# Which unit of a group TensorE turns, when u is turned, and the order of a load and a transpose on SyncE

## The reference, cut to what matters

```python
x = x + layernorm(attention(layernorm(x)))       # only the last 516 tokens have a context
def bitlinear(x, w_latent):
    scale = clip(mean(abs(w_latent), axis=1), 1e-5)
    tern  = clip(round(w_latent / scale), -1, 1)
    return x @ (tern * scale).T
h = bitlinear(x, w_fc) + gate * (x @ v.T @ fast_b.T @ u.T)      # 1024 -> 4096, low rank 16
out = bitlinear(relu(h) ** 2, w_proj)                           # 4096 -> 1024
x = x + layernorm(out)
```

## Time and profile before

| | us |
|---|---|
| median of 3 runs | 1076.35 (1075.03 to 1078.9) |
| the profiled execution's own time | 1073.45 |
| its span, slowest core (core 2) | 1071.9 |
| spans of the eight cores | 1067.5 to 1071.9 |
| TensorE busy, core 2 | 1007.4 (94%) |
| VectorE, ScalarE, GpSimd busy, core 2 | 562.9, 361.5, 48.6 |

### The profile page before, as it was taken

One profiled execution on the slowest core, in us unless ns is written; L12 is line 12 of the kernel. 1 busy time (PEld: TensorE's weight loads), 2 busy tenths in 40 slices (PEclk: granted clock), 3 DMA queues, 4 the chain that ended last, 5 costly groups with the idle time before them and its releaser, 6 DMA issues.

```text
span 1071.9 us, 14984 instructions; the slowest of 8 cores (1067.5 to 1071.9 us)
## 1 busy us (share of the span) xinstructions
PE 1007.4 (94%) x4933; PEld 455.6 (43%) x4933; DVE 562.9 (53%) x813; ACT 361.5 (34%) x697; POOL 48.6 (5%) x105
## 2 busy tenths in 40 slices
PE   3688969999999999999999999999999999999997
PEld 1233334444444444444444444445444444444443
DVE  3679878745654545453445445633445353544333
ACT  4678788530003431143212341124301332013200
POOL 1111121000001000000000000000000000000000
PEclk9999889999999999999999999999999999999999
DMA  8699999942564125710455124622145401411021
GB/s 271 167 247 257 208 241 203 205 104 79 152 163 109 55 50 113 163 48 8 75 136 109 50 36 95 141 63 62 47 111 138 79 21 30 118 50 40 1 66 53
DMA packets 106367, 116.93 MB, mean 109 GB/s; under 512 B 82333, under 2 KB 82589, under 8 KB 106292
## 3 DMA queue, kind: packets, MB, share of 16 engines
q1 hardware_dynamic: 102324, 103.64, 38.7%
q0 software_dynamic: 3728, 12.25, 6.2%
q10 hardware_dynamic: 240, 0.07, 0.0%
HBM read 87.79 MB, written 17.31 MB: 98 GB/s over the span
## 4 chain that ended last, share of the span: by engine, by line
PE 82%; DVE 5%; issue 4%; DMA 4%; ACT 2%; POOL 1%; SPq 1%; ACTq 0%; DVEq 0%; POOLq 0%
PE pjp L649 38%; PE fcb L632 31%; PE pjp L632 2%; PE xp L799 1%; PE xp L649 1%; PE xp L762 1%; PE fcb L649 1%; DVE below L1443 1%; ACT rpp L1030 1%; PE pt L632 1%; DMA r<-v 1%; DMA Sfc<-tern 1%; ACT absd L1070 1%; PE pjp L696 1%; POOL rthr L521 1%
## 5 line engine op out<-in xcount | busy, mean ns | idle before, releaser
L632 PE MATMUL fcb<-xnT,Sfc 128*128 128x512 bf16 x1792 | 410.0, 386 | 8.1 <-DVE r L1425 4.9
L649 PE MATMUL pjp<-Spj,r 128*128 128x512 fp8e4 x1664 | 365.1, 379 | 1.7 <-DVE r2b L1425 1.7
L632 PEld LDWEIGHTS fcb<-xnT,Sfc 128*128 128x128 bf16 x1792 | 172.0, 99 | 229.0 <-issue 39.1
L1425 DVE TENSOR_TENSOR r<-fcb,rpp 128x512 bf16<-128x512 f32 x192 | 131.3, 690 | 224.7 <-ACT rpp L1030 224.5
L649 PEld LDWEIGHTS pjp<-Spj,r 128*128 128x128 bf16 x1664 | 160.5, 98 | 194.5 <-issue 5.0
L1030 ACT ACTIVATE rpp<-fcb,hsc 128x512 f32<-128x512 f32 x192 | 130.4, 686 | 208.5 <-PE fcb L632 199.3
L993 ACT ACTIVATE lv<-mv,cvecs 128x1 f32<-128x1 f32 x64 | 18.7, 293 | 281.2 <-DVE mv L1370 204.8
L1360 DVE TENSOR_TENSOR xy<-pjp,oscb 128x512 f32<-128x512 f32 x60 | 41.3, 689 | 130.2 <-PE pjp L649 130.2
L649 PE MATMUL pjp<-Spj,r2b 128*128 128x512 fp8e4 x256 | 55.4, 379 | 0.0
L1365 DVE BATCH_NORM_STATS2 s<-xy 128x6 f32<-128x512 f32 x64 | 44.4, 694 | 9.4 <-DVE xy L1360 6.0
L632 PE MATMUL pjp<-xnT,Sfc 128*128 128x512 bf16 x176 | 42.0, 390 | 6.2 <-ACT rpp L1030 4.7
(11 more groups left out here) (181 smaller groups left out, 704.8 us busy)
## 6 DMA issues: line engine op xcount, KB each, us to landing
xy<-x SPq DMA_DIRECT2D x31, 512.0 KB, 4.4
out<-xy SPq DMA_DIRECT2D x31, 512.0 KB, 3.0
xs<-x SPq DMA_DIRECT2D x25, 512.0 KB, 4.6
xy<-wfc SPq DMA_DIRECT2D x16, 512.0 KB, 5.8
xy<-wpj SPq DMA_DIRECT2D x16, 512.0 KB, 5.9
stg<-wfc SPq DMA_DIRECT2D x10, 512.0 KB, 6.0
stg<-wpj SPq DMA_DIRECT2D x8, 512.0 KB, 4.9
xs<-wpj SPq DMA_DIRECT2D x8, 512.0 KB, 5.4
```

What stands on the lines that cost most here:

```text
L632: mm = te.matmul(bank, s_fc[:, dci * HF + hc * 128:dci * HF + hc * 128 + 128], xnT[:, dci * TT:(dci + 1) * TT], start=(dci == 0), stop=(dc ...
L649: mm = te.matmul(dst, squares(j)[:, hc * TT + s * 128: hc * TT + s * 128 + 128], spj_even[:, hc // 2, hc % 2, half * 512:half * 512 + 512] ...
L1425: ve.tensor_tensor(squares(j)[:, hc * TT:(hc + 1) * TT], bank, rpp[n % 2][:], ALU.mult).then_inc(v_r2, 1)
```

## The change

- `BY_PE` holds units 1, 5, ... 29 and 31: nine units in place of eight, and of each group the second in place of the fourth.
- In TensorE's steps 4, 8, ... 24, `ut` comes behind `low_rank(n + 3)` and not ahead of it.
- ScalarE copies a unit that TensorE has turned behind the step's `abssum` and not ahead of it.
- SyncE issues the load into a slot ahead of the transpose of the unit that freed it, for all units.
- The first 16 chunks stand in steps 35 to 47 and not 37 to 47.

```diff
-BY_PE = [n for n in range(NFU) if n % 4 == 3]
+BY_PE = [n for n in range(NFU) if n % 4 == 1 or n == NFU - 1]
...
-    CHUNKS[37 + 11 * c // 16 if c < 16 else 17 + 2 * c if c < 20 else 36 + c
+    CHUNKS[35 + 13 * c // 16 if c < 16 else 17 + 2 * c if c < 20 else 36 + c
...
                 sync.wait_ge(v_ab, m + 1)
-                turned(m)
                 if m in AFTER:
                     wload(AFTER[m])
+                turned(m)
...
                 if n == 0:
                     low_rank(2)
-                if n == 1 or (n > 1 and n % GRP == 0 and n + 4 < NFU):
-                    ut(n // GRP + 1)
+                if n == 1:
+                    ut(1)
                 if n + 3 < NFU:
                     low_rank(n + 3)
+                if n > 1 and n % GRP == 0 and n + 4 < NFU:
+                    ut(n // GRP + 1)
...
-                if n in BY_PE:
-                    evac(n)
                 if n in STATS:
                     rstd1(STATS[n])
...
                 for u in SUMS[n]:
                     abssum(u)
+                if n in BY_PE:
+                    evac(n)
```

## The result

Over four runs of each in turn on one chip, the kernel after took 1088.87 us in the median (1086.96 to 1089.65) and the kernel before 1077.2 (1075.03 to 1078.9). The ratio is 1.0107, with a 95% interval of 1.0083 to 1.0131: 11.7 us slower, where 4.0 had been forecast. A few executions of every kernel here are some per cent longer, with a lower clock on the cores of a die; the ratios and the means leave them out. The profiled execution took 1088.99.

What follows compares the result with a forecast made beforehand. Bound: a TensorE stream of fixed length from step 48, whose start VectorE's cuts set. On core 2, 4.6 - 1.1 - 0.9 + 1.0 = +3.6, plus 0.4 for the slowest core: +4.0, median 1080.4 us; 8-in-10 range 1070 to 1088.

Steps and rivals of the forecast that it cites:

- The stream behind step 48 is of fixed length: TensorE from step 48 on, 887.1 us on core 2: time lost ahead of it arrives at the end almost whole.
- Unit 12: VectorE's cut of unit 12 on core 2 comes at 67.0 instead of 70.41, 3.4 us gained; less on other cores.
- The series copy, unit, `fc`, low rank product: Four statistics groups: TensorE's unit waits for ScalarE's late copy of u; 13.5 us against 12.67, 0.85 us lost in each.
- The clock: 1.9 a group: TensorE's 3.1 us gap in each of four groups lowers the clock for a short spell, costing 1.9 us a group.
- Units 28 to 33, 1.1 gained: Unit 33's stop shrinks with one transpose less on the queue: 1.1 us gained, bounds 2.5 gained and 1 lost.
- 33 to 47, 0.9 gained: Chunks two steps sooner: units 33 to 47 take 38.5 us instead of 39.4, bounds 3 gained and 4 lost.
- Behind unit 47: 1.0 lost: Unit 47's transpose is issued 0.57 later, behind a 512 KB load: 1.0 us lost, bounds 0.6 and 2.5.
- The rival that built on it: `w_proj` part: transposes behind loads land 1.5 us later, stopping every third cut, 6.5 us more, 1086.9; chance 0.10.
- The slowest of eight: +0.4: At the end, all cores finish near core 2, the slowest 0.4 us above the mean.
- The clock holds: Rival: 3.1 us gaps in the four groups leave the clock alone, -4.0 us, 1072.3; chance 0.22.
- The copy in time: Rival: ScalarE's copy of u is not late, groups stay at 12.67, -7.5 us, 1068.9; chance 0.08.
- All cancels: Rival: unit 12's gain offsets 0.85 and half the spells, within a microsecond or two of before, 1077; chance 0.10.

Runs made afterwards that it cites:

- experiment 12: Kernel after, with one `fc` product repeated ahead of TensorE's unit in steps 13, 17, 21, 25 and the products of chunks 14 and 15 repeated: ratio 1.0029 to before.
- Experiment 11: Kernel before with the first 16 chunks in steps 35 to 47 and the products of chunks 14 and 15 made once more: ratio 1.0024 to before.
- experiment 10: Kernel before with only the first 16 chunks moved to steps 35 to 47: ratio 1.0047 to before.
- Experiment 4: Kernel after with the `fc` of unit n - 2 repeated ahead of TensorE's unit in steps 13, 17, 21, 25: 1081.4 us, ratio 1.0035 to before.
- experiment 2: Kernel before with only SyncE's load issued ahead of the transpose: ratio 1.0023 to before.
- experiment 8: Kernel before with the load ahead of the transpose, except for units 45, 46 and 47: ratio 0.9997 to before.
- experiment 3: Kernel after with ScalarE's `rstd1` at the end of its step, behind the copy of u: 1080.89 us, ratio 1.0020 to before.
- experiment 5: Kernel after with the first 16 chunks back in steps 37 to 47: ratio 1.0101 to before.
- experiment 1: Kernel after with SyncE's order and the chunks as before, leaving unit choice, `ut` order and ScalarE's copy changed: 1087.22 us, ratio 1.0087 to before.
- experiment 6: Kernel before with only u's turn moved behind the low rank product: 1075.73 us, ratio 0.9968 to before.
- experiment 7: Kernel after with TensorE's unit at the end of its step, behind `fc` and the low rank product: 1082.89 us, ratio 1.0048 to before.

## Why the prediction was right in its mechanism and wrong in its size

**The stream behind step 48 is of fixed length: wrong by 3 us.** I had said that a microsecond lost ahead of step 48 arrives at the end almost whole. It does, but the tail grew as well, from 887.1 to 890.1 us on core 2 and by 3.2 in the mean. On core 2, 1.5 us of the 3.0 are the two products at step 48 (their starts take 190.25 to 195.18, 4.93 for 3.45), and 1.3 are clock lost between 340 and 350 us, which no run ties to the change (last section). In the mean the two products make 1.9 of the 3.2. Over the kernels of the table it follows the wait at step 48: 888.5 to 889.6 us in the six where that wait is below 2 us, 890.4 and 890.5 where it is 3.1 and 3.4, 891.0 to 891.9 in the five where it is 5.0 to 6.4 (experiment 12, with 2.2 and 890.9, lost clock elsewhere as well). The two products themselves are longer by 0.0 to 0.4 us in the mean of the cores in those six, by 1.4 in the two and by 1.9 to 2.4 in the five. On core 4 the two products behind the wait are 3.57 + 2.96 for 1.89 + 1.89, 2.8 us more. Experiment 11 did nothing but fill this wait in experiment 10, and the lost clock and the tail went down with it. I had priced the later transpose as 1.0 us of delay and had not asked what a wait of 5 us does to the clock, though I had just asked that of the groups.

**Unit 12: 3.4 us gained, 67.0.** On core 2 it was cut at 65.05, 5.4 sooner; in the mean of the cores 1.8, as the forecast said of the others.

**The series copy, unit, `fc`, low rank product.** Right as a mechanism: gaps ahead of the unit in all 32 places (four groups on eight cores), each ended by the copy of u. Their sizes are 2.84 to 4.43 us for a forecast of 3.1; on six cores the first is the longest. 63.6 us in the mean, and 63.55 on core 2, stand where I had 61.8. (Four times 13.5 and 1.9 is 61.6 or 61.7 and not 61.8; that slip changes nothing.) Experiment 4, with the clock held, has 55.6, 13.9 for a group against my 13.5. With the clock, the first group of core 4 is 66.19 to 82.69, 16.5: the statistics end 7.2 behind the cut and not 6.75, since VectorE stops for 0.39 us on `Sfc<-tern` ahead of them, and the copy ends 3.8 behind them and not 3.54.

**The clock: 1.9 a group.** Right: 8.0 us over four groups, 2.0 each, by after less experiment 4. I took it that all four gaps of a core lower it; 27 of 32 did, so one that did cost 2.4 (8.0 x 8 / 27), and that two errors cancel here is luck again. The other five, all of 3.03 or 3.04 us, were followed by `fc` at 1.89, as on core 2:

```profile
109.58 0.61 PE L714 MATMUL pt<-identb,tern 128*128 128x128 bf16 x8 [3.04 <-ACT uTs L1088]
110.03 1.89 PE L632 MATMUL fcb<-xnT,Sfc 128*128 128x512 bf16 x8
```

So "none above 2.5 did" is not a bound: it held for the 7 gaps of before and fails for 5 of 32. Nor does the length alone decide: a gap of 3.03 us on core 4 was followed by the low clock, and so were gaps of 1.85 and 1.89 us of before (cores 5 and 6), below the range that I had counted. The spell on core 4 runs from 77.49 to 81.85, 4.4 us. By the rule of the Trainium skill, TensorE: Matmul & The Clock Gate, section "HAM oscillation — how this bites in real kernels", that a spell costs half its length, this is 2.2; the rows give (0.81 - 0.46) + (3.55 - 1.82) = 2.1 between starts, so trace and rule agree, and my lower estimate by it had too short a spell.

**Unit 28 at 128.8: right.** Core 2 has 128.60. That two errors cancelled there (unit 12 two us sooner, the groups two longer) is luck.

**Units 28 to 33, 1.1 gained, and 33 to 47, 0.9 gained.** On core 2, 0.6 and 0.8 gained (14.94 and 38.56; forecast for the latter 38.5). In the mean of the cores 0.5 gained and 0.2 lost.

**Behind unit 47: 1.0 lost.** A term that was mis-sized: 8.15 for 5.75 on core 2, 2.4 us, at its bound of 2.5 (1.9 in the mean of the cores). I had counted the load's 0.57 of issue and 0.4 for the company; the landing itself takes 1.0 to 1.3 longer in the middle (4.0 to 5.0 on core 4, 3.9 to 5.2 on core 3 in experiment 2). The Trainium skill, DMA: Bandwidth & Descriptors, section "Two DMAs through the same engine are not ordered", has descriptors of one queue overlapping; these landings, longer by much less than the 5.4 that a load takes, agree with that. The rival that built on it came half true. VectorE stops for `Spj<-ternp` 8 times and 5.7 us on core 4 where before shows one of 0.8, but units 33 to 47 take 39.1 us for 38.9, so as much is given back ahead of unit 47 (that it is the earlier loads that give it is not shown), and the price is paid at step 48.

**The slowest of eight: +0.4.** This is the term with the largest error in the profiled execution: core 4 ended 7.1 us behind core 2 (1087.4 to 1080.3). Core 2 lost 8.4 us and the seven others 10.0 to 18.8; core 4 lost 17.9, from 1069.5. Core 4's groups took 65.25 us, 12.1 more than its own of before, and its tail 7.2 more. Of the 7.1 us between the two cores, 1.1 stand at unit 12 already, 1.7 come in the groups and 4.6 in the tail: 1.2 at step 48, 1.6 between 340 and 360 us, 1.7 at 820 us. Where each group takes a fixed 16 us on every core none catches up, so I had no ground for "all end near core 2".

**The sum on core 2:** 4.4 at unit 28 - 0.6 - 0.8 + 2.4 + 3.0 = 8.4, for a forecast of 3.6. Of the 4.8 that are missing 2.9 are at step 48, 1.4 in the late transposes and 1.5 in the clock; 1.3 are the clock near 340 us, the rest are small terms. **The steps that failed are three. The term behind unit 47 was 1.0 and measured 2.4. The assumption ahead of all terms, that the stream behind step 48 keeps its length, was off by 3.0 on core 2 and 3.2 in the mean, of which 1.5 and 1.9 are the low clock behind the longer wait. And "all end near core 2", priced at 0.4 for the slowest core, measured 7.1: the one core that I had worked out won 5.4 us at unit 12, where the mean won 1.8.** Of these three, experiments 8, 10 and 11 bear out the late transposes and the clock at step 48; the clock lost at 340 and 820 us is in no way explained.

**The rivals.** The clock holds: refuted by the rows and by experiment 4, which made it true by hand and then measured +3.8 us in the end (1.0035), not -4.0, as the wait at step 48 stays (6.4 us). The copy in time: experiment 3 made this true for some of the gaps and came to +2.2 us; its groups took 13.9 us and not the rival's 12.67, and the wait at step 48 stays too (6.2 us). All cancels: the groups alone lost 10.4 us, and nothing made up for them.

**What stays open.** The new chunks cost 5 us alone (experiment 10) and nothing inside the change (experiment 5). Half of the 5 is the clock at step 48, which in after is lowered with either formula (3.4 and 5.8 us of wait); why units 33 to 47 lose 2 us with the new chunks in before and none in after isn't known. Nor is it known why units 33 to 47 take 2.2 us more with TensorE's part alone (experiment 1) and 2.0 less with the load first (experiment 2) but not in experiment 8, or where experiment 6 gains.

## What to carry to other kernels

Price a wait on TensorE twice, for its length and for the clock behind it, and do so at every wait that a change makes longer, the last one ahead of a solid stretch too. When an instruction is moved nearer to the copy that it waits for, read what stands ahead of that copy on its own engine: moving one call of ScalarE gave back 8 us here, and filling the gap with repeated products, 8 us as well. Where TensorE waits for a transpose, as at step 48 here, issue it ahead of the load: that took the 0.2% of experiment 2 back.

## What the runs showed of the hardware that I had not expected

**A lower clock without a gap, on all cores at once.** Windows of core 7 and core 0 of the kernel after, then of core 4 of both kernels, before first (stretch, its length; busy time and count of TensorE's matmuls and weight loads, VectorE, ScalarE, GpSimd; granted clock, DMA share, GB/s):

```profile
340.00:350.00 10.00, 10.00 (x43) 4.35 (x42) 6.61 (x10) 4.33 (x8) 0.00 (x0) 0.89 0.60 166
350.00:360.00 10.00, 10.00 (x47) 4.37 (x45) 5.58 (x10) 3.29 (x8) 0.53 (x1) 0.82 0.40 119
...
356.00:358.00 2.00, 2.00 (x10) 0.77 (x8) 1.93 (x3) 0.66 (x2) 0.11 (x1) 0.81 0.01 2
```
```profile
348.00:350.00 2.00, 2.00 (x9) 0.81 (x8) 0.69 (x1) 0.59 (x2) 0.00 (x0) 0.81 0.62 229
```
```profile
320.00:360.00 40.00, 38.61 (x190) 17.54 (x189) 21.84 (x37) 16.16 (x29) 4.24 (x8) 1.00 0.35 96
```
```profile
320.00:360.00 40.00, 40.00 (x179) 17.69 (x178) 19.59 (x31) 8.82 (x18) 3.32 (x6) 0.93 0.55 132
```

TensorE is busy throughout and yet has 0.89 and 0.82, and 179 matmuls stand for 190. In windows of 2 us this is one level, 0.81, which is neither of the two that the spells above go between: core 7 has it from 346 to 358 us, core 0 from 346 to 350. All eight cores show it in the window from 340 us, cores 4 to 7 in the next one too: 0.9 to 1.3 us of clock lost on cores 0 to 3, 2.8 or 2.9 on cores 4 to 7. Before and experiments 1 to 10 lose nothing between 210 and 700 us, experiments 4, 5 and 7 with all or nearly all of the change among them; 11 and 12 lose 0.5 there in the mean, near 340 us and on cores 4 to 7 alone. So I don't put it down to the change, and no run says what brings it about; cores 4 to 7 have it together and longer than cores 0 to 3, so it seems to come by die. It makes part of core 4's long tail, 894.7 against 890.1 on core 2; another 1.7 us of clock is lost by core 4, and none by core 2, at 820 us.

**A spell near 800 us in every kernel.** TensorE waits there for a transpose of the attention, core 0 of before:

```profile
800.00 0.60 PE L840 MATMUL xp<-PT,Vt 128*64 128x128 bf16 x4 [2.78 <-DMA PT<-Pb]
```

Core 0 then has 0.68 in the window from 800 to 810 us, 3.5 us of clock in all. Core 2 waited 2.19 us at the same place and kept 1.00. In before three cores of eight lose nothing there; in after four; in experiments 2, 3, 4, 5, 8 and 10 none gets off. This may be a part of why the profiled execution of before was a short one.
